# A rope product's halves are swapped by ScalarE on the way out of PSUM, instead of by VectorE in its two multiplies

## The chip, the cores and the metric

The kernel runs on one core of a Trainium2 chip. The metric is the device time of the execution in microseconds, the median of several runs. One more execution is taken by the hardware profiler, and all rows below are from that one.

## What is computed

One attention block and one feed-forward block over 1024 tokens of width 512, each behind a layer norm and with a residual. The attention has 32 query heads of width 128 in 8 groups; keys K and values V are shared by the four heads of a group. Each head has besides them a latent key and value of its own (LK, LV), and attends twice with the same query: to K, V and to LK, LV. The queries, the keys and the latent keys pass through the rotary embedding (rope), which is where the change lies:

```
def _rotate_half(x):
    h = x.shape[-1] // 2
    return jnp.concatenate([-x[..., h:], x[..., :h]], axis=-1)

def _apply_rope(x, cos, sin):
    return x * cos[None, None] + _rotate_half(x) * sin[None, None]
...
q = _apply_rope(q, cos, sin)
k = _apply_rope(k, cos, sin)
lk = _apply_rope(lk, cos, sin)
...
attn = _causal_attn(q, k, v, SCALE)
lat = _causal_attn(q, lk, lv, SCALE)
...
return attn @ w_o + lat @ w_lo
```

## The kernel before

Every engine runs its own list of instructions, written out by hand in the order in which it is to work, and waits on semaphores. The matmuls are in fp32r with each operand split into a high and a low half (`_hi`, `_lo`), so a product takes three matmuls (L433 to L435). ScalarE makes the high half by a copy (L721 is the one line of all its copies), and VectorE or GpSimd subtracts it from the source for the low half (L997 and L1070 on VectorE, L1213 on GpSimd).

**A head** has four windows: w = 0 and 1 are K, V for the first and the second half of the queries (512 tokens each), w = 2 and 3 the same for LK, LV. A window has 4 or 8 blocks of keys (slots s). In each slot TensorE computes score tiles of the next window, one *piece* of other work, the transposes of the exponentials (L496) and the product of a block with the values in bankO. VectorE takes the row maxima (L991), ScalarE the exponentials (L780). Transposed blocks pass as PT_hi (ScalarE) and PT_lo (VectorE), or PTD_hi and PTD_lo for the last block of a window. The transposes of block j + 2 wait until PT_lo of block j is written, because they write the same bankT.

**Pieces** are the projections of what the next window or head needs. Each writes 512 columns of PSUM, in bankX or in the second half of scores[1]. LK0 and LK1 (the two halves of the tokens) come in w = 0, slots 0 and 1; Q0 of the next head in w = 2, slot 3; Q1 in w = 3, slot 0, in the same bankX right after it. In the last head of a group K0, K1 and V0 of the next group take slots 0 to 2 of w = 2 as well. Before TensorE writes a bank again, it waits (`bank_x_taken`) until the last piece in it was read; for a rope piece this is the semaphore `rope_raw`.

**A rope product** passes through four engines. ScalarE copies the bank to one of three slots of `rot` and raises `rope_raw` (`rope_take`). VectorE (`rotate`) multiplies each half of the partitions by sine and writes it to the other half of `rot_half`, which has two places (L1007, L1008), and raises `rope_half`. GpSimd multiplies `rot` by cosine in place (L1219), adds `rot_half` (L1221) and raises `rope_sum`. ScalarE copies the high half to QT, KT or LKT (`rope_high`), GpSimd subtracts for the low half (L1213) and raises `rope_lo`, for which the score tiles wait. In ScalarE's list the take of LK stands in front of the slot's PT_hi and exponentials; that of Q and K stands behind the exponentials and in front of PT_hi. In VectorE's list the rotation of Q stands in front of PT_lo of the same slot; that of LK and K stands one slot later, behind PT_lo. There are 144 such products: 64 LK, 64 Q and 16 K, four of them before the first head.

Of the kernel before, what the change touches and what calls it, by code (L numbers as in the profile page):

```python
# [9 lines left out]
ALU = mybir.AluOpType  # L10
# [6 lines left out]
H, KVH, HD = 32, 8, 128  # L17
# [5 lines left out]
HALF = HD // 2  # L23
# [6 lines left out]
RING = 3  # L30
# [70 lines left out]
def attn_ffn_kernel(nc, x_in, w_q, w_k, w_v, w_o, w_lq, w_lk, w_lv, w_out_latent, W, b, A, B, router_W, router_b,  # L101
                    cos_in, sin_in, mask_in, ident_in, pick_in,
                    averaged_in, out, inverses):
    with ExitStack() as ctx:
        def sb(name, shape, dt=F32):
            return ctx.enter_context(nc.sbuf_tensor(name, shape, dt))
# [5 lines left out]
        def sem(name):  # L112
            return ctx.enter_context(nc.semaphore(name))
# [3 lines left out]
        sin = sb("sin", [P, S])  # L117
# [17 lines left out]
        rot_half = sb("rot_half", [P, 2, CH])  # L135
        rot = sb("rot", [P, RING, CH])
# [22 lines left out]
        banksX = [bankX[:, :], scores[1][:, 1, :]]  # L159
# [13 lines left out]
        rope_raw, rope_half, rope_cos = sem("rope_raw"), sem("rope_half"), sem("rope_cos")  # L173
        rope_sum, rope_lo, o_lo, w_lo, cleared = (sem("rope_sum"), sem("rope_lo"), [sem("o_lo0"), sem("o_lo1")], sem("w_lo"),
                                                  sem("cleared"))
# [542 lines left out]
        def _(act):  # L718

            def copy(place, src):  # L720
                return act.activation(place, src, ACT.Copy)  # L721
# [36 lines left out]

                weights_hi(None, no % 2, g * (LOADS_PER_GROUP // 2) + (no // 2 + 1), places)

            def rope_take(n_x, no, slot, bank=0):

                if not (isinstance(no, int) and no < RING):
                    act.wait_ge(rope_lo, no - (RING - 1))
                act.wait_ge(x_ready, n_x)
                copy(rot[:, slot, :], banksX[bank] if isinstance(bank, int) else bank).then_inc(rope_raw, 1)

            def rope_high(no, slot, place):
                act.wait_ge(rope_sum, no + 1)
# [29 lines left out]
            def group_of_heads(g, last):  # L799
                for hh, w, more in windows(g, last):  # L800
# [3 lines left out]
                    for s in range(BLOCKS[w]):  # L804
                        name, n = pieces_of(w, hh, more).get(s, ("", 0))
                        if name == "LK":
                            rope_take(n_piece(g, hh, w, s), rope_no(g, hh, name, n), rope_no(0, hh, name, n) % RING,
                                      piece_bank(hh, w, s, more))
# [7 lines left out]
                        if name in ("Q", "K"):  # L816
                            rope_take(n_piece(g, hh, w, s), rope_no(g, hh, name, n), rope_no(0, hh, name, n) % RING,
                                      piece_bank(hh, w, s, more))
# [63 lines left out]
            def first_take(p):  # L882
                rope_take((1, 2, 5, 6)[p], p, p % RING, four[p % 2])
# [45 lines left out]
        def _(dve):  # L929
# [70 lines left out]
            def rotate(no, slot, n, place=None):  # L1000

                half = n if place is None else place
                if not (isinstance(no, int) and no < 2):
                    dve.wait_ge(rope_sum, no - 1)
                dve.wait_ge(rope_raw, no + 1)
                t = slice(n * CH, (n + 1) * CH)
                dve.tensor_tensor(rot_half[0:HALF, half, :], rot[HALF:HD, slot, :], sin[HALF:HD, t], ALU.mult)  # L1007
                dve.tensor_tensor(rot_half[HALF:HD, half, :], rot[0:HALF, slot, :], sin[0:HALF, t], ALU.mult)\  # L1008
                    .then_inc(rope_half, 1)

            def value_copy(n_x, n, bank=0):
                dve.wait_ge(x_ready, n_x)
# [13 lines left out]
            def piece(g, hh, w, s, name, n, bank):  # L1026
                n_x = n_piece(g, hh, w, s)
                if name in ROPE:
                    rotate(rope_no(g, hh, name, n), rope_no(0, hh, name, n) % RING, n)
                elif name in ("V", "LV"):  # L1030
                    value_copy(n_x, n, bank)
                elif name in ("VT", "LVT"):

                    value_lo(vt_no(g, hh, name, n) + 3, V if name == "VT" else LV, n, bank)
                else:
                    add_out(n_x, n_free(g, hh, w, s), n + (TPC if name == "OUT1" else 0), bank)
# [93 lines left out]
            for i in range(TPC, NT):  # L1130
                normalised_lo(0, i)
            rotate(0, 0, 0, 0)
            rotate(1, 1, 0, 1)
            latent_lo(0)
            dve.wait_ge(mask_made, 1)
# [66 lines left out]
            for n in range(2):  # L1202
                dve.wait_ge(f_hi, ND + 3 + n)
                t = slice(n * CH, (n + 1) * CH)
# [114 lines left out]
def shape_constants():  # L1319

    inv_freq = (1.0 / THETA ** (np.arange(0, HD, 2, dtype=np.float32) / HD)).astype(np.float32)
    freqs = np.outer(np.arange(S, dtype=np.float32), inv_freq).astype(np.float32)
    cos = np.tile(np.cos(freqs).T, (2, 1)).astype(np.float32)
    sin = np.concatenate([np.sin(freqs).T, -np.sin(freqs).T], 0).astype(np.float32)
    mask = np.zeros((P, S), np.float32)
    mask[:, S - P:] = np.where(np.tril(np.ones((P, P), bool)), 0.0, MASKED)
    pick = (np.arange(P)[:, None] // R == np.arange(E)[None, :]).astype(np.float32)
    token = np.arange(NT)[None, :] * P + np.arange(P)[:, None]
    averaged = ((token >= Q_START) & (token < Q_STOP)).astype(np.float32)
    return {"cos": cos, "sin": sin, "mask": mask, "ident": np.eye(P, dtype=np.float32), "pick": pick,  # L1330
            "averaged": averaged}
# [19 lines left out]
```

## Time and profile before

| | us |
|---|---|
| median of 3 runs (2121.29 to 2122.29) | 2121.59 |
| the profiled execution | 2121.26 |
| its span, first to last instruction | 2119.5 |
| TensorE busy | 2066.4 (97%) |
| VectorE busy | 1531.2 (72%) |
| ScalarE busy | 1203.0 (57%) |
| GpSimd busy | 894.4 (42%) |

TensorE's granted clock is 0.998 of full speed over the span. PE in the rows is TensorE's matmul, PEld its weight load, DVE VectorE, ACT ScalarE, POOL GpSimd. Ends of matmuls are modelled and overlap the next one. One ordinary head lasts about 60 us, and the last of a group about 73.

### The profile page before, as it was taken

The numbers are of one execution on the slowest core, as the hardware profiler recorded it, in microseconds if no ns is written. First come the engines' busy times: TensorE is split into PE (matmuls) and PEld (weight loads), VectorE is DVE, ScalarE is ACT, GpSimd is POOL, SyncE is SP. The second block draws the span as 40 slices with busy tenths as digits, with TensorE's granted clock in tenths as the row PEclk, the third lists the DMA queues.
The fourth block names the chain that finished last, engine by engine and source line by source line (L and its number), as shares of the span: only waits on it lengthen the run. The fifth ranks groups of instructions, "written<-read, shape, count | busy, mean of one in ns | idle before, by whom it ended". The sixth has DMA issues, their size and how long they took to land.

```text
span 2119.5 us, 32469 instructions
## 1 busy us (share of the span) xinstructions
PE 2066.4 (97%) x11236; PEld 1754.4 (83%) x11236; DVE 1531.2 (72%) x2946; ACT 1203.0 (57%) x2507; POOL 894.4 (42%) x691
## 2 busy tenths in 40 slices
PE   6999999999999999999999999999999999999989
PEld 5888888888888888888888888888888888888877
DVE  7777777776777677777677767777677777777775
ACT  4566555565566555566556555556646555555641
POOL 4433453444544353444443345444354345444411
PEclk9999999999999999999999999999999999999999
DMA  2111111111111111111111111111111111111121
GB/s 97 42 37 38 45 32 40 29 42 47 31 34 40 33 41 37 36 42 32 37 42 37 35 47 32 27 42 37 47 31 37 42 27 47 31 42 36 38 51 40
DMA packets 101937, 83.72 MB, mean 39 GB/s; under 512 B 28296, under 2 KB 73992, under 8 KB 101776
## 3 DMA queue, kind: packets, MB, share of 16 engines
q1 hardware_dynamic: 101776, 81.65, 15.1%
q8 instruction: 91, 1.49, 0.3%
q14 instruction: 70, 0.57, 0.1%
HBM read 79.26 MB, written 2.36 MB: 39 GB/s over the span
## 4 chain that ended last, share of the span: by engine, by line
PE 69%; DVE 15%; POOL 6%; issue 6%; ACT 4%; DMA 0%; SPq 0%; ACTq 0%; DVEq 0%
PE scores L433 9%; PE scores L435 9%; PE scores L434 9%; PE bankT L496 7%; PE bankX L433 6%; PE bankX L435 6%; PE bankX L434 6%; PE bankO L433 5%; PE bankO L435 5%; PE bankO L434 5%; DVE rot_half L1008 4%; DVE rot_half L1007 4%; DVE PT_lo L997 2%; POOL rot L1219 2%; POOL rot L1221 2%
## 5 line engine op out<-in xcount | busy, mean ns | idle before, releaser
L721 ACT ACTIVATE PT_hi<-bankT 128x512 fp32r<-128x512 f32 (+2 forms) x640 | 336.3, 532 | 389.1 <-PE bankO L435 326.9
L997 DVE TENSOR_TENSOR PT_lo<-bankT,PT_hi 128x512 fp32r<-128x512 f32 (+2 forms) x640 | 386.7, 607 | 194.7 <-ACT PT_hi L721 189.7
L780 ACT ACTIVATE probs<-probs,nmax 128x128 f32<-128x128 f32 (+7 forms) x512 | 395.5, 774 | 134.3 <-DVE nmax L991 133.7
L991 DVE CUSTOM_DVE_ANT_0 probs<-scores,mask 128x128 f32<-128x128 f32 (+7 forms) x512 | 381.3, 750 | 55.5 <-PE scores L435 54.4
L496 PE MATMUL bankT<-ident,probs 128*128 128x128 f32 x2304 | 379.1, 273 | 22.2 <-DVE PT_lo L997 20.0
L496 PEld LDWEIGHTS bankT<-ident,probs 128*128 128x128 f32 x2304 | 285.2, 140 | 90.6 <-DVE PT_lo L997 35.6
L1213 POOL TENSOR_TENSOR OT_lo<-o_raw,OT_hi 128x512 fp32r<-128x512 f32 x64 | 99.9, 1561 | 417.6 <-ACT OT_hi L721 417.6
L1219 POOL TENSOR_TENSOR rot<-rot,cos 128x512 f32<-128x512 f32 x144 | 186.2, 1293 | 199.4 <-DVE rot_half L1008 199.4
L721 ACT ACTIVATE OT_hi<-o_raw 128x512 fp32r<-128x512 f32 x128 | 147.0, 1148 | 145.5 <-DVE o_raw L1062 145.5
L1221 POOL TENSOR_TENSOR rot<-rot,rot_half 128x512 f32<-128x512 f32 x144 | 204.1, 1417 | 11.3
L1007 DVE TENSOR_TENSOR rot_half<-rot,sin 64x512 f32<-64x512 f32 x144 | 110.0, 764 | 85.4 <-ACT rot L721 81.7
L1008 DVE TENSOR_TENSOR rot_half<-rot,sin 64x512 f32<-64x512 f32 x144 | 153.7, 1067 | 2.0
L721 ACT ACTIVATE rot<-bankX 128x512 f32<-128x512 f32 x140 | 83.3, 595 | 109.7 <-PE bankX L435 108.7
L433 PE MATMUL scores<-LKT_hi,QT_lo 128*128 128x384 f32 (+4 forms) x384 | 138.4, 361 | 2.4
L433 PE MATMUL bankO<-PT_hi,LV_lo 128*128 128x512 f32 (+2 forms) x320 | 136.0, 425 | 0.3
L433 PE MATMUL bankO<-PT_hi,V_lo 128*128 128x512 f32 (+2 forms) x320 | 136.1, 425 | 0.0
L433 PE MATMUL scores<-KT_hi,QT_lo 128*128 128x384 f32 (+4 forms) x384 | 133.8, 348 | 1.5 <-POOL KT_lo L1213 1.2
L1024 DVE TENSOR_TENSOR acc<-scores,acc 128x512 f32<-128x512 f32 x130 | 89.6, 690 | 62.7 <-PE scores L435 59.9
L435 PE MATMUL scores<-KT_hi,QT_hi 128*128 128x384 f32 (+4 forms) x384 | 132.0, 344 | 0.0
L435 PE MATMUL scores<-LKT_hi,QT_hi 128*128 128x384 f32 (+4 forms) x384 | 131.9, 343 | 0.0
L434 PE MATMUL scores<-KT_lo,QT_hi 128*128 128x384 f32 (+4 forms) x384 | 131.7, 343 | 0.0
L434 PE MATMUL scores<-LKT_lo,QT_hi 128*128 128x384 f32 (+4 forms) x384 | 131.7, 343 | 0.0
(254 smaller groups left out, 5170.5 us busy)
## 6 DMA issues: line engine op xcount, KB each, us to landing
inv_b<-inverses SPq DMA_DIRECT2D x128, 256.0 KB, 3.9
stage<-in_L_attn_w_q SPq DMA_DIRECT2D x32, 256.0 KB, 4.8
stage<-in_L_attn_w_lv SPq DMA_DIRECT2D x32, 256.0 KB, 2.8
stage<-in_L_attn_w_o SPq DMA_DIRECT2D x32, 256.0 KB, 4.9
stage<-in_L_attn_w_lo SPq DMA_DIRECT2D x32, 256.0 KB, 2.6
acc<-in_L_attn_hidden_states SPq DMA_DIRECT2D x8, 256.0 KB, 4.8
stage<-in_L_attn_w_k SPq DMA_DIRECT2D x8, 256.0 KB, 5.1
stage<-in_L_attn_w_v SPq DMA_DIRECT2D x8, 256.0 KB, 5.4
```

Of the source, the lines that this page charges most:

```text
L433: pe.matmul(place, left[1], right[0], start=start, stop=False)
L434: pe.matmul(place, left[0], right[1], start=False, stop=False)
L435: return pe.matmul(place, left[0], right[0], start=False, stop=stop)
L496: mm = pe.transpose(bankT[j % 2][:, t * P:(t + 1) * P], probs[c][:, at:at + P], ident[:, :])
L721: return act.activation(place, src, ACT.Copy)
L780: act.activation(prob_tile(c, t), prob_tile(c, t), ACT.Exp, bias=nmax[:, c, t:t + 1], scale=-1.0, accum_out=rsum[:, c, t:t + 1]).then_inc( ...
L991: dve.tensor_tensor_reduce(place, src, tile_view(mask[:, S - width:S], c), -SCALE, -MASKED, ALU.add, ALU.min, nmax[:, c, t:t + 1]).then_in ...
L997: dve.tensor_tensor(pt_place(1, hh, w, j), bankT[j % 2][:, block_columns(c, j):CH], f32(pt_place(0, hh, w, j)), ALU.subtract).then_inc(pt_ ...
L1007: dve.tensor_tensor(rot_half[0:HALF, half, :], rot[HALF:HD, slot, :], sin[HALF:HD, t], ALU.mult)
L1008: dve.tensor_tensor(rot_half[HALF:HD, half, :], rot[0:HALF, slot, :], sin[0:HALF, t], ALU.mult)\
L1219: pool.tensor_tensor(rot[:, slot, :], rot[:, slot, :], cos[:, chunk(n)], ALU.mult).then_inc(rope_cos, 1)
L1221: pool.tensor_tensor(rot[:, slot, :], rot[:, slot, :], rot_half[:, half, :], ALU.add).then_inc(rope_sum, 1)
```

## The change

ScalarE reads the bank three times: the upper half of the partitions to the lower half of `rot_half`, the lower half to the upper, and then the whole to `rot` as before, where `rope_raw` is raised. VectorE multiplies all of `rot_half` by sine in one instruction, in place. The sine table has its sign in the other half. The wait for `rope_sum` of two products before, which protects the place in `rot_half`, moves from VectorE to ScalarE.

```diff
-            def rope_take(n_x, no, slot, bank=0):
-
-                if not (isinstance(no, int) and no < RING):
+            def rope_take(n_x, no, slot, bank=0, place=None):
+
+                half = no % 2 if place is None else place
+                src = banksX[bank] if isinstance(bank, int) else bank
+                if no >= 2:
+                    act.wait_ge(rope_sum, no - 1)
+                if no >= RING:
                     act.wait_ge(rope_lo, no - (RING - 1))
                 act.wait_ge(x_ready, n_x)
-                copy(rot[:, slot, :], banksX[bank] if isinstance(bank, int) else bank).then_inc(rope_raw, 1)
+                copy(rot_half[0:HALF, half, :], src[HALF:HD, :])
+                copy(rot_half[HALF:HD, half, :], src[0:HALF, :])
+                copy(rot[:, slot, :], src).then_inc(rope_raw, 1)
...
                 half = n if place is None else place
-                if not (isinstance(no, int) and no < 2):
-                    dve.wait_ge(rope_sum, no - 1)
                 dve.wait_ge(rope_raw, no + 1)
                 t = slice(n * CH, (n + 1) * CH)
-                dve.tensor_tensor(rot_half[0:HALF, half, :], rot[HALF:HD, slot, :], sin[HALF:HD, t], ALU.mult)
-                dve.tensor_tensor(rot_half[HALF:HD, half, :], rot[0:HALF, slot, :], sin[0:HALF, t], ALU.mult)\
-                    .then_inc(rope_half, 1)
+                dve.tensor_tensor(rot_half[:, half, :], rot_half[:, half, :], sin[:, t], ALU.mult).then_inc(rope_half, 1)
...
-    sin = np.concatenate([np.sin(freqs).T, -np.sin(freqs).T], 0).astype(np.float32)
+    sin = np.concatenate([-np.sin(freqs).T, np.sin(freqs).T], 0).astype(np.float32)
```

## Rows read from the trace of the kernel before

**Rows 1.** The page: busy time of each engine, share of the span, instructions.

```profile
PE 2066.4 (97%) x11236; PEld 1754.4 (83%) x11236; DVE 1531.2 (72%) x2946; ACT 1203.0 (57%) x2507; POOL 894.4 (42%) x691
```

**Rows 2.** Waits: who waited <- for whom: us in total, times, longest.

```profile
PE bankT L496 <- DVE PT_lo L997: 20.0, 32, 1.1
...
PEld scores L433 <- POOL LKT_lo L1213: 16.4, 32, 0.5
...
PEld bankX L433 <- ACT rot L721: 3.0, 7, 0.4
```

**Rows 3.** Instructions on tile rot_half: duration in ns min/median/max, first and last start.

```profile
L1007 DVE TENSOR_TENSOR rot_half<-rot,sin x144: 686/687/1810, 26.1 to 2008.1; 64x512 f32<-64x512 f32 x144
L1008 DVE TENSOR_TENSOR rot_half<-rot,sin x144: 684/685/1690, 26.8 to 2008.8; 64x512 f32<-64x512 f32 x144
```

**Rows 4.** Timeline of TensorE, 907 to 918: start us, duration us, instruction [idle before <-releaser].

```profile
909.09 0.48 PE L433 MATMUL bankX<-xnT_hi,Wq_lo 128*128 128x512 f32 x1
...
911.70 0.39 PE L435 MATMUL bankX<-xnT_hi,Wq_hi 128*128 128x512 f32 x1
...
915.14 0.40 PE L434 MATMUL scores<-Wlo_lo,OT_hi 128*128 128x512 f32 x1
915.37 0.40 PE L435 MATMUL scores<-Wlo_hi,OT_hi 128*128 128x512 f32 x1
916.27 0.66 PE L496 MATMUL bankT<-ident,probs 128*128 128x128 f32 x4 [0.50 <-DVE PT_lo L997]
...
917.46 0.28 PE L433 MATMUL scores<-KT_hi,QT_lo 128*128 128x256 f32 x1
```

**Rows 5.** Timeline of ScalarE, the same stretch.

```profile
908.20 0.60 ACT L721 ACTIVATE rot<-bankX 128x512 f32<-128x512 f32 x1 [0.60 <-PE bankX L435]
908.69 1.33 ACT L721 ACTIVATE PT_hi<-bankT 128x512 fp32r<-128x512 f32 x2
...
912.74 0.60 ACT L721 ACTIVATE rot<-bankX 128x512 f32<-128x512 f32 x1
...
914.39 0.60 ACT L721 ACTIVATE PT_hi<-bankT 128x512 fp32r<-128x512 f32 x1 [0.54 <-PE bankO L435]
914.89 0.62 ACT L721 ACTIVATE QT_hi<-rot 128x512 fp32r<-128x512 f32 x1
```

**Rows 6.** Timeline of VectorE, the same stretch.

```profile
909.61 0.69 DVE L1008 TENSOR_TENSOR rot_half<-rot,sin 64x512 f32<-64x512 f32 x1
910.32 0.69 DVE L997 TENSOR_TENSOR PT_lo<-bankT,PT_hi 128x512 fp32r<-128x512 f32 x1
910.93 0.68 DVE L1062 TENSOR_TENSOR o_raw<-bankO,inv_b 128x512 f32<-128x512 f32 x1
...
915.52 1.29 DVE L997 TENSOR_TENSOR PT_lo<-bankT,PT_hi 128x512 fp32r<-128x512 f32 x2
```

**Rows 7.** Timeline of GpSimd, the same stretch.

```profile
915.59 1.27 POOL L1213 TENSOR_TENSOR QT_lo<-rot,QT_hi 128x512 fp32r<-128x512 f32 x1 [2.54 <-ACT QT_hi L721]
```

**Rows 8.** Timeline around LK1, 933 to 944, of ScalarE, VectorE and TensorE.

```profile
933.35 0.60 ACT L721 ACTIVATE rot<-bankX 128x512 f32<-128x512 f32 x1 [1.46 <-PE bankX L435]
...
934.15 0.29 DVE L997 TENSOR_TENSOR PTD_lo<-bankT,PTD_hi 128x128 fp32r<-128x128 f32 x1 [0.30 <-ACT PTD_hi L721]
...
935.89 1.23 DVE L991 CUSTOM_DVE_ANT_0 probs<-scores,mask 128x1024 f32<-128x1024 f32 x1
...
938.23 0.60 PE L496 MATMUL bankT<-ident,probs 128*128 128x128 f32 x4
...
943.13 0.40 PE L435 MATMUL bankO<-PT_hi,V_hi 128*128 128x512 f32 x1
943.60 0.39 PE L433 MATMUL scores<-LKT_hi,QT_lo 128*128 128x256 f32 x1
```

**Rows 9.** Timeline at the end of a group: K1's copy, V's first matmul.

```profile
1029.57 0.60 ACT L721 ACTIVATE rot<-bankX 128x512 f32<-128x512 f32 x1
...
1030.22 0.50 PE L433 MATMUL bankX<-xnT_hi,Wv_lo 128*128 128x512 f32 x1
```

## The prediction

> **What bounds the kernel now.** I read the page's busy line first, then the waits, then the instructions of one head in order of time. TensorE is busy 97% of the span and VectorE 72% [rows 1], so the question for every edit is whether it moves a matmul. A record of TensorE overlaps the next one: a 512-column matmul is booked with 0.40 us, but the next starts 0.23 us after it (915.14 to 915.37) [rows 4]. So a hole in TensorE is read from start to start, not from its busy time. In the heads the holes that matter are few. Once a head transposes wait for VectorE's PT_lo, 32 times for 20.0 us [rows 2]; in the head at 908 that is a start at 916.27 where 915.60 (915.37 + 0.23) was possible, 0.67 us [rows 4]. Once a head the first latent score waits for GpSimd's LKT_lo, 32 times [rows 2]: 943.13 to 943.60 is 0.47 where 0.23 is the step, 0.24 us lost [rows 8]. In front of bankX, waits for ScalarE's copy are only 7, and short [rows 2]. The heads repeat this closely; the head at 908 stands for the 24 heads that fetch a next query without new keys, and 7 more also make K and V.
>
> The second thing to see is how near to TensorE the copy already is. Of a head's four rope products, Q0 and Q1 follow each other through the same bankX. Q0's copy runs 908.20 to 908.80, and TensorE starts Q1 there at 909.09 [rows 5, 4]. Where it does wait (1029.57 + 0.60, matmul at 1030.22 [rows 9], once per group) the signal takes 0.05. The slack is then 0.24 us. The same gap of 0.28 or 0.29 is there at 30 of the 31 Q0 (the first at 89.89, the last at 1979.12), 0.05 at one. LK0, LK1 and K0 leave more room than two copies take.
>
> **VectorE's part.** Two 64x512 multiplies of 0.69 us go, 144 times each; that is their median, and single ones last up to 1.8 [rows 3], stretched when GpSimd works at the same time. One 128x512 multiply comes. The trace has the same operation at half the partitions for 0.69, as long as 128x512 PT_lo, so partitions are free and I price it at 0.69. The old pair does not overlap its neighbours: 909.61 to 910.32 is a step of 0.71, while PT_lo to o_raw is 0.61 for 0.69 [rows 6]. I take 0.61 for the new one, so VectorE gets back 1.42 - 0.61 = 0.80 us a product. Bounds: 0.71 gained if it keeps the long step, 1.7 where it escapes a stretch. It is in place and also uses two SBUF inputs, so a stretch to 1.7 stays possible. The Trainium skill (VectorE: DVE Perf Modes, Two Vector instructions with no wait between them) says that an instruction whose start quadrant differs from the last one's waits for everything before it; the steps of 0.71 and 0.61 agree, and it says nothing of ScalarE.
>
> **ScalarE's part.** Two 64x512 copies from PSUM come in front of the one that was there, and `rope_raw`, which frees bankX and starts VectorE, comes only with the third. A copy takes 0.60 [rows 5]; by VectorE's half-height rows a half is no cheaper than a whole. ScalarE's copies overlap when they start at partition 0: 908.20 to 908.69, a step of 0.49 [rows 5]. No row shows ScalarE moving between partitions 0 and 64. The price of the pair lies between 2 x 0.49 = 0.98 (overlap kept) and 2 x 0.62 = 1.24 (none, as VectorE's rows with just these halves). I take 1.24, because the row with the same change of partitions is the nearer one; both ends stay in. The Trainium skill (ScalarE: Activation LUTs, What ACT_TABLE_LOAD costs) gives an immediate-operand ACTIVATE 186 ns + 0.833 ns an element and an overlap of about 93 ns back to back, whatever the partitions; as an estimate that is 0.52 a copy, 1.04 for the pair, and the sum would be near the first rival's. The added wait for `rope_sum` of two products before costs nothing in the heads: that product was added up several us earlier; VectorE loses the same wait.
>
> **Q0 and Q1, with 1.24.** Q0's third copy ends 908.20 + 1.24 + 0.60 = 910.04, TensorE gets bankX at 910.09 instead of 909.09: a new hole of 1.00 us, ahead of the whole Q1 projection, its score and output work. Now what is late next. Q1's last matmul ended 911.70 + 0.39; with 1.00 and 0.10 for the signal ScalarE can take it at 913.19. ScalarE itself is late too: VectorE's multiply starts 1.24 later but gives 0.80 back, so o_raw and OT_hi come 0.44 later, and the take, 912.74 before [rows 5], starts near 913.3. Its three copies end at 913.3 + 1.84 = 915.15. VectorE multiplies at 915.25 and reaches PT_lo at 915.86 instead of 915.52 [rows 6]. Before, TensorE's transposes followed PT_lo's start by 0.75, so they can start at 916.61; TensorE by itself is there at 915.60 + 1.00 = 916.60. So the old hole of 0.67 disappears in the new one, and 0.34 us remain.
> Behind it stands Q0's high and low half. ScalarE's PT_hi at 914.39 waited for TensorE; it is now pushed to 915.53 by the copies, QT_hi from 914.89 to 916.03 [rows 5], GpSimd's QT_lo (0.70 behind QT_hi's start, 1.27 long [rows 7]) to 916.73, ending 918.00. The score that reads it began at 917.46 [rows 4] and now begins at 918.05: 0.59 us late in all. 24 x 0.59 = 14.2 us.
>
> **LK1.** Before it ScalarE idles 1.46 us, which hides LK0's extra copies. LK1's own move PTD_hi behind them: VectorE's PTD_lo from 934.15 to about 935.38 (933.35 + 1.24 + 0.49 + 0.27 + 0.03), and the 1024-wide maximum follows 1.74 - 0.80 = 0.94 later, at 936.32 instead of 935.89 [rows 8]. Its exponential is late by 0.43; the transposes that read it (938.23, four of them [rows 8]) have perhaps 0.1 to spare. TensorE loses about 0.33 and then no longer waits for LKT_lo, 0.24: net 0.09, 32 x 0.09 = 3 us.
>
> **K1, V and the group ends (7).** V's first matmul already waits for K1's copy [rows 9] and moves by the whole 1.24. Q0 to Q1 adds up to 1.00. Holes of the same stretch (the largest kind of wait for PT_lo is 1.1 [rows 2]) swallow part; between 1.2 and 2.2 I take 1.4: 10 us. Start: TensorE works without a hole while the first products are taken, nothing. End: no ropes.
>
> **Sum.** 14.2 + 3 + 10 = 27 us. The profiled execution took 2121.26 with a span of 2119.5, 0.3 below the median of 2121.59. Forecast 2148, 1.3% slower.
>
> **Rivals.**
> *ScalarE overlaps the three copies* (0.98). For it: every pair of ScalarE copies in the trace overlaps. Against: VectorE's pair with these halves does not. Q1 then starts 0.74 late, the transposes 0.07, and the score behind QT_lo 0.19: 24 x 0.19 = 4.6. At LK1 the maximum is 0.17 late, less than slack and LKT_lo's 0.24 together: 32 x -0.17 = -5. Group ends 7 x 1.25 = 9. Time 2130.
> *VectorE's relief decides, faster.* The mechanism is the 0.80 us returned in front of PT_lo. It wins only if the two half copies together cost under the 0.24 of slack; then the holes close, 24 x 0.67 + 7 x 1.2 + 32 x 0.24 = 32 us, 2089. The balance tips near 0.8 for the pair, 0.4 a copy. For it: only half of the partitions are written. Against: half-height VectorE instructions cost as much as full ones.
> *No change.* The pair at about 0.8, or the halves overlapped and the group ends swallowing all of it: 2118 to 2126.
> *ScalarE becomes a second bound.* If in-place multiplies stretch to 1.7 beside GpSimd where the old pair ran at 0.69, VectorE gains nothing, maxima and PT_lo are 0.3 to 0.8 later in each head: 10 to 25 us on top, 2158 to 2172.
>
> **How the numbers follow.** Forecast case 50%, with a range of its own 2140 to 2157; overlapped copies 29%; no change 7%; faster 8%; second bound 6%. A difference under 0.2% cannot be told from none here. Range: down to 2125, below the overlapped case's own error of 5 us, and up to 2158. Faster 0.08, same 0.07, slower 0.85.
>
> **What would show it.** In the new trace: three ScalarE rows of bankX for each product, and their step (0.62 or 0.49); VectorE's multiply once, 0.69 long; first matmul of Q1 waiting for ScalarE's rot about 1.0 us, 31 times; the wait of transposes for PT_lo nearly gone; a new wait of the scores for QT_lo; the wait for LKT_lo gone. The forecast is wrong if a half copy is much cheaper than 0.49, if QT_lo is not late, or if VectorE's stretches grow.

## The result and the profile after

The changed kernel takes 2147.24 us (median of 4, 2146.86 to 2147.62) against 2121.44 for the kernel before in the same comparison: ratio 1.0123, 95% interval 1.0105 to 1.014. The forecast was 2148, range 2125 to 2158. The profiled execution has a span of 2145.6 instead of 2119.5.

The page, part 1, busy time of each engine [rows 1 before]:

```profile
PE 2074.2 (97%) x11236; PEld 1758.5 (82%) x11236; DVE 1350.2 (63%) x2802; ACT 1378.4 (64%) x2795; POOL 879.6 (41%) x691
```

The change did what it says: 181 us of work left VectorE and 175 came to ScalarE. The two engines are nearly as busy as each other now, and the kernel is slower. The waits tell why (who <- for whom: us in total, times, longest) [rows 2 before]:

```profile
PEld bankX L433 <- ACT rot L721: 42.2, 38, 1.7
...
PE bankX L433 <- ACT rot L721: 32.6, 38, 1.3
PEld scores L433 <- POOL QT_lo L1215: 21.9, 31, 1.4
...
PEld scores L433 <- DVE nmax L997: 15.0, 58, 0.5
...
PE scores L433 <- POOL QT_lo L1215: 6.9, 7, 1.0
...
PEld bankT L496 <- DVE PT_lo L1003: 0.7, 2, 0.5
```

TensorE waited for ScalarE's copy 7 times before, now 38 times (31 Q1 and 7 V). The wait for PT_lo, once a head before, is gone, and so is the one for LKT_lo. A wait for QT_lo has come, 31 times. Score tiles wait for a row maximum (nmax) in 58 records instead of 26; the row of the kernel before is:

```profile
PEld scores L433 <- DVE nmax L991: 6.2, 26, 0.5
```

The same place as [rows 4 to 7], one ordinary head, timeline of TensorE (start, duration, instruction, idle before and its releaser):

```profile
919.55 0.60 PE L496 MATMUL bankT<-ident,probs 128*128 128x128 f32 x4
920.90 0.50 PE L433 MATMUL bankX<-xnT_hi,Wq_lo 128*128 128x512 f32 x1 [0.75 <-ACT rot L721]
...
927.18 0.39 PE L435 MATMUL scores<-Wlo_hi,OT_hi 128*128 128x512 f32 x1
927.41 0.60 PE L496 MATMUL bankT<-ident,probs 128*128 128x128 f32 x4
...
928.31 0.40 PE L435 MATMUL bankO<-PT_hi,LV_hi 128*128 128x512 f32 x1
928.77 0.39 PE L433 MATMUL scores<-KT_hi,QT_lo 128*128 128x256 f32 x1
929.00 0.28 PE L434 MATMUL scores<-KT_lo,QT_hi 128*128 128x256 f32 x1
```

and of ScalarE, VectorE and GpSimd there:

```profile
919.04 1.20 ACT L721 ACTIVATE rot_half<-bankX 64x512 f32<-64x512 f32 x2 [0.62 <-PE bankX L435]
920.25 0.60 ACT L721 ACTIVATE rot<-bankX 128x512 f32<-128x512 f32 x1
920.75 1.08 ACT L721 ACTIVATE PT_hi<-bankT 128x512 fp32r<-128x512 f32 x2
...
926.73 0.62 ACT L721 ACTIVATE QT_hi<-rot 128x512 fp32r<-128x512 f32 x1
...
920.88 0.69 DVE L1011 TENSOR_TENSOR rot_half<-rot_half,sin 128x512 f32<-128x512 f32 x1 [4.05 <-ACT rot L721]
921.49 0.68 DVE L1003 TENSOR_TENSOR PT_lo<-bankT,PT_hi 128x512 fp32r<-128x512 f32 x1
...
926.49 1.28 DVE L1003 TENSOR_TENSOR PT_lo<-bankT,PT_hi 128x512 fp32r<-128x512 f32 x2
...
927.42 1.29 POOL L1215 TENSOR_TENSOR QT_lo<-rot,QT_hi 128x512 fp32r<-128x512 f32 x1 [3.10 <-ACT QT_hi L721]
```

The two half copies take 1.20 (919.04 to 920.25), with no overlap; the copy behind them gives way after 0.50, as before. TensorE gets bankX 1.86 us after the first copy starts, before 0.89. From there on the transposes at 927.41 start with no hole behind 927.18, and the score at 928.77 has one of 0.23.

At the end of a group, TensorE's timeline [rows 9 before]:

```profile
1042.97 0.50 PE L433 MATMUL bankX<-xnT_hi,Wv_lo 128*128 128x512 f32 x1 [1.34 <-ACT rot L721]
...
1062.40 0.39 PE L433 MATMUL scores<-KT_hi,QT_lo 128*128 128x256 f32 x1 [0.98 <-POOL QT_lo L1215]
```

Around LK0 and LK1, ScalarE's, VectorE's and TensorE's [rows 8 before]:

```profile
941.76 1.21 ACT L721 ACTIVATE rot_half<-bankX 64x512 f32<-64x512 f32 x2
...
943.47 0.38 ACT L721 ACTIVATE PT_hi<-bankT 128x256 fp32r<-128x256 f32 x1
...
944.77 1.20 ACT L721 ACTIVATE rot_half<-bankX 64x512 f32<-64x512 f32 x2
...
943.88 0.42 DVE L1003 TENSOR_TENSOR PT_lo<-bankT,PT_hi 128x256 fp32r<-128x256 f32 x1 [2.11 <-ACT PT_hi L721]
944.22 0.95 DVE L997 CUSTOM_DVE_ANT_0 probs<-scores,mask 128x768 f32<-128x768 f32 x1
...
946.78 0.29 DVE L1003 TENSOR_TENSOR PTD_lo<-bankT,PTD_hi 128x128 fp32r<-128x128 f32 x1 [0.59 <-ACT PTD_hi L721]
946.99 0.68 DVE L1011 TENSOR_TENSOR rot_half<-rot_half,sin 128x512 f32<-128x512 f32 x1
947.59 1.22 DVE L997 CUSTOM_DVE_ANT_0 probs<-scores,mask 128x1024 f32<-128x1024 f32 x1
...
945.23 0.19 PEld L433 LDWEIGHTS scores<-KT_hi,QT_lo 128*128 128x128 f32 x1 [0.26 <-DVE nmax L997]
```

and LK0 before the change:

```profile
930.24 0.58 ACT L721 ACTIVATE rot<-bankX 128x512 f32<-128x512 f32 x1
...
931.51 0.96 DVE L991 CUSTOM_DVE_ANT_0 probs<-scores,mask 128x768 f32<-128x768 f32 x1
...
933.73 0.39 PE L433 MATMUL scores<-KT_hi,QT_lo 128*128 128x512 f32 x1
```

Before, the maximum over 768 columns started 1.27 us behind LK0's copy and had ended, 932.47 at the latest, more than 1 us ahead of the next score tile, which did not wait. Now LK0's copies stand in front of PT_hi, PT_lo and this maximum. It starts 2.46 us behind the first of them, and the score tile waits for it.

From one Q0 copy to the next in ScalarE's timeline, the four heads of a group took 59.7, 59.7, 69.0 and 64.4 us; now 60.2, 60.2, 70.7 and 64.7. An ordinary head lost 0.5 us, a whole group 3.1. From the first Q0 to the last the loss is 23 us; of the other 3, 1.2 lie ahead of the first (its copy starts at 91.06 instead of 89.89) and the rest behind the last. These 3 cannot simply be put down to the change. TensorE's granted clock ahead of the first Q0 is 1.00 of full speed (2.4 GHz) in the trace before and 0.98 in the one after, and behind the last 0.96 and 0.95; between them it is 1.00 in both. Run 6, whose edit leaves the start alone, has 0.98 there too and is as late: the last matmul of the first Q0 projection starts at 90.7 us, at 90.5 in the changed kernel and at 89.4 before.

### The profile page after: what moved, and what is told of

Its sections match the earlier page's. It is cut to its first block, busy times and chain, and to the rows that moved or that the text cites. A ratio compares the mean times of both kernels' runs of the same rounds, so it can differ in the third digit from the quotient of the medians.

```text
span 2145.6 us, 32472 instructions
## 1 busy us (share of the span) xinstructions
PE 2074.2 (97%) x11236; PEld 1758.5 (82%) x11236; DVE 1350.2 (63%) x2802; ACT 1378.4 (64%) x2795; POOL 879.6 (41%) x691
## 4 chain that ended last, share of the span: by engine, by line
PE 85%; ACT 7%; DVE 3%; issue 2%; POOL 2%; DMA 0%; SPq 0%; ACTq 0%; DVEq 0%
PE scores L433 12%; PE scores L435 11%; PE scores L434 11%; PE bankT L496 9%; PE bankX L433 8%; PE bankX L435 7%; PE bankX L434 7%; PE bankO L435 6%; PE bankO L433 6%; PE bankO L434 5%; ACT rot_half L721 3%; POOL QT_lo L1215 2%; ACT rot L721 1%; ACT OT_hi L721 1%; ACT QT_hi L721 1%
## 5 line engine op out<-in xcount | busy, mean ns | idle before, releaser
L721 ACT ACTIVATE PT_hi<-bankT 128x512 fp32r<-128x512 f32 (+2 forms) x640 | 331.4, 533 | 334.2 <-PE bankO L435 274.4
L721 ACT ACTIVATE rot_half<-bankX 64x512 f32<-64x512 f32 x280 | 166.2, 594 | 73.4 <-PE bankX L435 66.4
L1011 DVE TENSOR_TENSOR rot_half<-rot_half,sin 128x512 f32<-128x512 f32 x144 | 113.2, 786 | 144.2 <-ACT rot L721 144.2
L1223 POOL TENSOR_TENSOR rot<-rot,rot_half 128x512 f32<-128x512 f32 x144 | 196.7, 1366 | 11.3
L433 PE MATMUL scores<-KT_hi,QT_lo 128*128 128x384 f32 (+4 forms) x384 | 140.7, 366 | 10.1 <-POOL QT_lo L1215 6.9
L1026 DVE TENSOR_TENSOR acc<-scores,acc 128x512 f32<-128x512 f32 x130 | 89.6, 689 | 62.4 <-PE scores L435 59.7
L1215 POOL TENSOR_TENSOR QT_lo<-rot,QT_hi 128x512 fp32r<-128x512 f32 x64 | 82.6, 1290 | 110.5 <-ACT QT_hi L721 110.5
```

Source lines behind the costliest of these rows:

```text
L433: pe.matmul(place, left[1], right[0], start=start, stop=False)
L1011: dve.tensor_tensor(rot_half[:, half, :], rot_half[:, half, :], sin[:, t], ALU.mult).then_inc(rope_half, 1)
L1215: return pool.tensor_tensor(place, src, f32(hi), ALU.subtract)
L1223: pool.tensor_tensor(rot[:, slot, :], rot[:, slot, :], rot_half[:, half, :], ALU.add).then_inc(rope_sum, 1)
```

## The experiments

Each was measured beside the kernel before, on the same chip as it; ratios are to it, with their 95% intervals. Where an ordinary head is given and nothing else is said, it is counted in TensorE's timeline from the last matmul of one Q0 projection to that of the next, 59.7 us in the kernel before.

**1. VectorE's part alone.** One multiply, one copy; the halves are not swapped.

```diff
-                dve.tensor_tensor(rot_half[0:HALF, half, :], rot[HALF:HD, slot, :], sin[HALF:HD, t], ALU.mult)
-                dve.tensor_tensor(rot_half[HALF:HD, half, :], rot[0:HALF, slot, :], sin[0:HALF, t], ALU.mult)\
-                    .then_inc(rope_half, 1)
+                dve.tensor_tensor(rot_half[:, half, :], rot[:, slot, :], sin[:, t], ALU.mult).then_inc(rope_half, 1)
```

> VectorE's part alone: one 128x512 multiply of rot by sine, without the swap of halves; ScalarE takes the bank with one copy, as before. Theory (a late bank and late copies cost the time, VectorE's relief is real but covered): with the relief and no added copies the waits of the transposes for PT_lo and of the scores for LKT_lo close, 24 x 0.67 + 7 x 1.2 + 32 x 0.24 = 32 us, so 2089 (2085 to 2096). Rival (VectorE is off TensorE's path, its relief is worth nothing): 2121, as before.

Measured: 2096.83 us, ratio 0.9879 (0.9864 to 0.9894). VectorE's relief is worth 24 us, so the rival falls. It is 8 short of 2089 and 1 outside the theory's range, and the waits name what came in its place:

```profile
PEld scores L433 <- POOL QT_lo L1211: 22.0, 31, 1.4
```

**2. ScalarE's part alone.** The half copies go to a spare tile, VectorE works as before.

```diff
+                if no >= 2:
+                    act.wait_ge(rope_sum, no - 1)
+                copy(spare[0:HALF, no % 2, :], src[HALF:HD, :])
+                copy(spare[HALF:HD, no % 2, :], src[0:HALF, :])
                 copy(rot[:, slot, :], src).then_inc(rope_raw, 1)
```

> ScalarE's part alone: the two half copies go to a spare tile, VectorE rotates with its two multiplies as before. Theory: the copies cost more than the whole change, because nothing is given back: at Q1 the transposes come 1.9 us late (24 x 1.9 = 46), at LK1 the exponential is 1.2 late (32 x 1.1 = 36), at a group's end about 3 (7 x 3 = 22): 2220 (2195 to 2240). Rival (the whole loss is TensorE's wait for the bank, 31 x 1.0): 2150, like the changed kernel.

Measured: 2225.13 us, ratio 1.0481 (1.0463 to 1.0498). The waits:

```profile
PEld bankT L497 <- DVE PT_lo L1003: 47.2, 40, 1.7
PEld bankX L434 <- ACT rot L722: 41.0, 38, 1.6
PEld bankT L497 <- ACT probs L786: 33.6, 36, 1.2
```

The copies alone cost 104 us, four times the change; the time is inside the theory's range. The bank is the smaller part of it. An ordinary head takes 62.7 us, 3.0 more than before. From start to start in TensorE's timeline, 0.96 of these are the bank, 0.71 a longer wait for PT_lo, 0.94 the exponential behind LK1, and most of the rest OT_lo and the score tile behind LK0, 0.2 each. The same 38 waits for the bank are in the changed kernel; the waits for PT_lo and for the exponential are not (2 and 5 records), and the difference between the two kernels is the 0.8 us a product that VectorE saves.

**3. Whole copies instead of halves.** As many copies and twice the elements, but all from and to partition 0; the halves are not swapped.

```diff
-                copy(rot_half[0:HALF, half, :], src[HALF:HD, :])
-                copy(rot_half[HALF:HD, half, :], src[0:HALF, :])
+                copy(rot_half[:, half, :], src)
+                copy(spare[:, no % 2, :], src)
```

> The changed kernel, but the two half copies are whole copies of 128 partitions from and to partition 0 (the halves are not swapped, the second goes to a spare tile): as many instructions, twice the elements, no change of partitions. Theory (a ScalarE copy that starts at other partitions than the last cannot overlap it, 0.61 a step instead of 0.49): steps of 0.49, 0.25 us less for each product, near 2131 (2127 to 2136). Rival (three reads of one bank, or the count of copies, make the step 0.61): 2147, as changed.

Measured: 2129.34 us, ratio 1.0039 (1.0026 to 1.0052), as the theory says. ScalarE's timeline:

```profile
911.68 0.60 ACT L722 ACTIVATE rot_half<-bankX 128x512 f32<-128x512 f32 x1 [0.62 <-PE bankX L436]
912.17 0.59 ACT L722 ACTIVATE spare<-bankX 128x512 f32<-128x512 f32 x1
912.65 0.60 ACT L722 ACTIVATE rot<-bankX 128x512 f32<-128x512 f32 x1
```

The steps are 0.49 and 0.48. Three reads of one bank in a row overlap, so the rival falls. Each copy lasts 0.60 with 64 partitions or 128; the lost overlap costs 0.24 us a product and 18 us over the kernel, two thirds of the whole loss. The run takes away two things at once, the move between partitions 0 and 64 and the half height. That the move is the one that costs the overlap is argued and not shown: no run has half copies that start where the last one did.

**4. Q1 in the other bank.**

```diff
-            return (sorted(pieces_of(w, hh, more)).index(s) + (w == 1)) % 2 if w in (1, 3) else 0
+            return (sorted(pieces_of(w, hh, more)).index(s) + (w == 1 or more)) % 2 if w in (1, 3) else 0
```

> The changed kernel, but Q1 (and with it every piece of the fourth window, in turn) goes to the other bank, so that TensorE doesn't wait for Q0's copies. Theory (behind the bank stands a chain of the same length, ScalarE's three copies of Q1, then PT_lo and QT_hi): the wait of 0.75 for the bank goes, and nearly the same time comes back as waits for PT_lo and QT_lo: 2143 to 2147. Rival (the bank wait is the cost): 31 x 0.9 = 28 us less, 2119.

Measured: 2137.92 us, ratio 1.0078 (1.0063 to 1.0093), between the two, 5 below the theory's range. TensorE's timeline of an ordinary head has three short waits where there was one for the bank:

```profile
920.31 0.47 PE L433 MATMUL bankX<-Wo_hi,OT_lo 128*128 128x512 f32 x1 [0.16 <-DVE OT_lo L1072]
...
922.20 0.66 PE L496 MATMUL bankT<-ident,probs 128*128 128x128 f32 x4 [0.27 <-DVE PT_lo L1003]
...
923.74 0.39 PE L433 MATMUL scores<-KT_hi,QT_lo 128*128 128x256 f32 x1 [0.18 <-POOL QT_lo L1215]
```

From one QT_hi to the next an ordinary head takes 60.15 us, against 60.2 in the changed kernel: there the time came back entirely, as the theory says, and the rival, 28 us less, falls. A group end is shorter by about 0.9, where I had counted nothing, and that makes 6 of the 9 us.

**5. The kernel before, with VectorE's rotation of Q1 behind PT_lo.**

```diff
-                        if s in here and here[s][0] not in ("LK", "K"):
+                        if s in here and here[s][0] not in ("LK", "K") and here[s] != ("Q", 1):
                             piece(g, hh, w, s, *here[s], piece_bank(hh, w, s, more))
                         if s + 2 < BLOCKS[w]:
                             block_lo(g, hh, w, s + 2)
+                        if s in here and here[s] == ("Q", 1):
+                            piece(g, hh, w, s, *here[s], piece_bank(hh, w, s, more))
```

> The kernel before, with VectorE's rotation of Q1 behind PT_lo of the same slot instead of in front of it; nothing of the change. Theory (in an ordinary head TensorE lost 0.67 us to PT_lo behind this rotation, and QT_lo is next, 0.2 to 0.4 later than it would then be wanted, as in the run of VectorE's part alone): 24 x 0.4 = 10 and about 5 at the group ends, 2106 (2100 to 2112). Rival (the hole only moves to a later block, whose PT_lo is now behind the rotation): 2121.

Measured: 2119.59 us against 2122.21, ratio 0.9988 (0.9978 to 0.9997): the order alone is worth nearly nothing, and the time is 8 us above the theory's range. The theory was right in what comes next and wrong in its size; the score now waits for QT_lo and gives back 0.64 of the 0.73 us that the transposes no longer lose:

```profile
916.04 0.39 PE L433 MATMUL scores<-KT_hi,QT_lo 128*128 128x256 f32 x1 [0.37 <-POOL QT_lo L1215]
```

**6. The same, and QT_hi one slot earlier.**

```diff
-            highs = [{(0, 3): ("LK", 0), (1, 0): ("LK", 1), (3, 1): ("Q", 0), (3, 3): ("Q", 1)} for _ in range(GROUP)]
-            highs[GROUP - 1].update({(2, 3): ("K", 0), (3, 0): ("K", 1)})
+            highs = [{(0, 3): ("LK", 0), (1, 0): ("LK", 1), (3, 0): ("Q", 0), (3, 3): ("Q", 1)} for _ in range(GROUP)]
+            highs[GROUP - 1].update({(2, 3): ("K", 0), (3, 0): ("K", 1), (3, 1): ("Q", 0)})
```

> The last kernel, and ScalarE makes QT_hi of Q0 one slot earlier in ordinary heads, in front of PT_hi of the next block instead of behind it. Theory (QT_lo is what is late next): the waits for QT_lo go there, 24 x 0.25 = 6 us less than the last one, near 2099 (2094 to 2105). Rival (QT_lo is not binding without the relief): as the last one.

Measured: 2122.58 us, ratio 1.0003 (0.9993 to 1.0012), 3 us above run 5, where 6 less were expected: a miss. The hole moved once more, to the transposes one slot later, which wait for the next PT_lo, now behind the rotation:

```profile
918.97 0.55 PE L496 MATMUL bankT<-ident,probs 128*128 128x128 f32 x3 [0.51 <-DVE PT_lo L997]
```

That was the rival of run 5. While VectorE needs 1.4 us for Q1 at this place, each of the three orders that were tried puts something of the stretch behind it.

**7. The changed kernel with its late steps moved.** Q1 in the other bank (run 4) and VectorE's order of run 5; in Q1's slot ScalarE makes PT_hi and Q0's QT_hi in front of the copies.

```diff
+                        if (name, n) == ("Q", 1):
+                            block_hi(g, hh, w, s + 2)
+                            if hh < GROUP - 1:
+                                act.wait_ge(scored, tiles_made(g, hh, w))
+                                rope_high(rope_no(g, hh, "Q", 0), rope_no(0, hh, "Q", 0) % RING,
+                                          QT[0][:, (hh + 1) % 2, 0:CH])
                         if name in ("Q", "K"):
```

> The changed kernel with its three late things moved: Q1 in the other bank, and in Q1's slot PT_hi and Q0's QT_hi in front of ScalarE's copies, PT_lo in front of VectorE's multiply. Theory (the change costs by where the copies stand, ScalarE has the time for them): the waits for bank, PT_lo and QT_lo of ordinary heads go, V's wait for K1's copies stays, 7 x 1.3: about 2108 (2100 to 2118). Rival (the added 175 us of ScalarE's work cost wherever they stand): over 2130.

Measured: 2121.58 us against 2122.21, ratio 0.9998 (0.9988 to 1.0007). The whole loss of the change is gone with ScalarE's work still there, so the rival falls; but the kernel is almost 4 us above the theory's range, 13 above its 2108, and not faster than before. Part of what stays is at the group's end, TensorE's timeline:

```profile
1030.95 0.50 PE L433 MATMUL bankX<-xnT_hi,Wv_lo 128*128 128x512 f32 x1 [1.34 <-ACT rot L721]
...
1049.52 0.38 PE L433 MATMUL scores<-KT_hi,QT_lo 128*128 128x256 f32 x1 [0.98 <-POOL QT_lo L1223]
```

The larger part is in the ordinary heads, which I had not foreseen. They take 59.5 us; in run 10, which has VectorE's relief without the copies, they take 58.5. The difference stands at three places of TensorE's timeline: 0.4 at the output product that reads OT_lo, 0.2 at the transposes behind Q1, 0.2 at the score tile behind LK0. The first is shown here:

```profile
855.35 0.47 PE L433 MATMUL bankX<-Wo_hi,OT_lo 128*128 128x512 f32 x1 [0.16 <-DVE OT_lo L1078]
```

Q0's copies make o_raw, a head's output before it is split, start 3.04 us behind the first of them instead of 2.73, and OT_hi and OT_lo follow it.

**8. The change for LK alone.** Q and K as before; the sign of their sine product is the other one.

```diff
-                copy(rot_half[0:HALF, half, :], src[HALF:HD, :])
-                copy(rot_half[HALF:HD, half, :], src[0:HALF, :])
+                if swap:
+                    copy(rot_half[0:HALF, half, :], src[HALF:HD, :])
+                    copy(rot_half[HALF:HD, half, :], src[0:HALF, :])
```

> The change for LK0 and LK1 alone (64 of 144 products); Q and K are taken and rotated as before (the sign of their sine product is the other one). Theory: 32 x 0.09 = 3 us over the kernel before, 2124 (2119 to 2129), the wait for LKT_lo gone and a small one for the exponential in its place. Rival (each product's copies cost alike): 64/144 of 26 us = 12, 2133.

Measured: 2120.50 us against 2122.21, ratio 0.9991 (0.9982 to 1.0001), inside the theory's range and clear of the rival. 64 of the 144 products cost nothing, if not a little less than nothing. The waits show two effects that nearly cancel: the 32 records of a wait for LKT_lo are gone, and those for a row maximum rise from 26 to 57:

```profile
PEld scores L433 <- DVE nmax L998: 14.4, 57, 0.5
```

Behind the first scores of a head, the rest of it takes 49.6 us instead of 49.7, and so it does in the changed kernel. The loss belongs to Q and K.

**9. The changed kernel of run 7, but K as before.** VectorE rotates K0 and K1 in two multiplies, GpSimd subtracts for them.

```diff
-                                      piece_bank(hh, w, s, more))
+                                      piece_bank(hh, w, s, more), swap=name == "Q")
...
-                            rope_add(*k_no[0], 0)
-                            rope_add(*k_no[1], 1)
+                            rope_add(*k_no[0], 0, op=ALU.subtract)
+                            rope_add(*k_no[1], 1, op=ALU.subtract)
```

> The last kernel with the change in its new places (Q1 in the other bank, PT_hi, QT_hi and PT_lo in front of it), but K0 and K1 are taken with one copy and rotated by VectorE in two multiplies as before the change, and GpSimd subtracts instead of adds for them, because the sine table has the other sign. Theory (what was left of the change's cost there is V's wait for K1's copies, 1.34 a group): 7 x 1.2 = 8 us less than that kernel's 2121.6, 2113 (2110 to 2117), faster than the kernel before by 0.4%. Rival (that wait is swallowed by the wait for QT_lo at the group's end, 0.98 there): 2120 to 2122.

Measured: 2113.36 us against 2120.15, ratio 0.9961 (0.9947 to 0.9974), as the theory says. It computes what the kernel before does and is faster than it and than the changed kernel. The waits for bankX are down to a few short ones:

```profile
PEld bankX L433 <- ACT rot L721: 3.4, 8, 0.4
```

**10. VectorE's part alone, and QT_hi one slot earlier** (the edits of runs 1 and 6; halves not swapped).

> VectorE's part alone (one multiply without the swap of halves, one copy by ScalarE), and ScalarE makes QT_hi of Q0 one slot earlier in ordinary heads. Theory (the part alone stayed at 2097 instead of 2089 because the scores then wait for QT_lo, 24 x 0.3): those waits go, 7 us less, 2090 (2086 to 2093). Rival (PT_hi, now behind QT_hi, makes PT_lo of the next block late, as it did without VectorE's relief): 2097.

Measured: 2085.91 us against 2120.15, ratio 0.9838 (0.9825 to 0.9851). That is 4 below the theory and just below its range. The 8 us missing in run 1 were the wait for QT_lo of ordinary heads, which take 58.5 us instead of run 1's 58.9; its records fall from 31 to the 7 of the group ends:

```profile
PEld scores L433 <- POOL QT_lo L1211: 9.9, 7, 1.4
```

The edit of run 6, worth nothing on its own, is worth 8 to 10 us once the rotation is short.

## Why the prediction was right, step by step

The time is 0.8 us from the forecast, and the likeliest case is the one that happened. That it came so close is luck: the heads lost 23 us where 27 were forecast, and the 3 us outside them, where nothing was forecast, go with a lower granted clock at the two ends of the kernel. Two terms were off by 6 and 2 us in opposite directions.

*ScalarE's price.* The choice of 1.24 for the two half copies over 0.98 decided between the forecast and 2130. Measured 1.20; run 3, which has the 0.98, gave 2129. The 1.24 was taken from VectorE's rows for the same halves; the trace after shows ScalarE losing its overlap on them too. The Trainium skill (ScalarE: Activation LUTs, What ACT_TABLE_LOAD costs) says that ACTIVATEs back to back overlap by about 93 ns. It names no condition on partitions. Run 3's copies agree with it, 0.60 long and 0.49 or 0.48 apart; the half copies of the changed kernel do not overlap at all.

*VectorE's price.* 0.61 a step: 920.88 to 921.49. Its median is 0.69; 9 of the 144 last over 0.9, up to 1.69, each while GpSimd is at work, and the mean is 0.79. The case of the second bound did not come.

*Q0 and Q1*, counted at 0.59 a head. The bank came 0.97 late (counted 1.00). PT_lo was only 0.13 late (0.34), from the first copy 7.45 us instead of 7.32; TensorE by itself was later than that, so it made no difference. QT_lo was late as described. From Q0's first copy to the first score with the new query it was 9.26 us before and is 9.73, 0.47 late where 0.59 were counted. Behind this wait the next matmul starts 0.23 later (928.77 to 929.00) and not 0.12 as before, which nobody had counted. So TensorE is 0.59 late in all when it goes on: 10.58 us from the last matmul of Q0's projection to the last of that score instead of 9.99. The 24 x 0.59 = 14.2 us came out, by two errors that cancel.

*LK0 and LK1*, counted at 0.09. This term has the wrong sign. The 1024-wide maximum was 0.28 late instead of 0.43, counted from LK1's first copy, and the transposes behind its exponential lost 0.03 us and not 0.33. LK0's copies, put at nothing because ScalarE idles behind them, cost 0.2 by way of the earlier maximum at 944.22. Against both stand 0.34 that TensorE no longer loses for LKT_lo (0.24 at the score and 0.10 at the matmul behind it). A head gains 0.1: -3 us where +3 were forecast. Run 8, with nothing but these products changed, has the same 0.1. The first rival's 2130, which run 3 met with 2129, hid errors of the same kind: 0.38 instead of 0.19 for Q0 and Q1, -0.31 instead of -0.17 for LK.

*Group ends*, counted at 1.4 and 0.09. A group lost 3.1 us, three ordinary heads 1.5 of it, so 1.6, or 1.7 without LK's gain. V's first matmul is 1.23 late (its wait is 1.34 as a record); the wait for QT_lo, 0.98, which I used for ordinary heads only, is here too and replaces the old one for PT_lo. 7 of them make 12, where 10 were forecast. 14 - 3 + 12 = 23 us, and the remaining 3 lie before the first Q0 and behind the last, where I had counted nothing.

*The faster rival* was right about its mechanism, and its condition, a pair of half copies under 0.24 us, was not met: runs 1 and 10 show 24 us behind VectorE's relief alone and 34 with QT_hi moved as well, where 32 were worked out. What the copies cost with nothing given back is the 104 us of run 2. Neither number can be read from the sum of 26: the parts overlap on the same waits, and 104 - 24 is not 26.

What stays open: whether the half height or the move between partitions takes ScalarE's overlap; what the places of run 7 would do for the kernel before, all together, since only runs 5 and 6 tried two of them there; and whether a swap without ScalarE could reach the 2086 of run 10.

## What to carry to other kernels

Where an engine's copy frees a PSUM bank for TensorE, price an added read of the bank by the slack between the copy's end and the next matmul into it, not by the engine's load: ScalarE was at 57% and had the time, 0.24 us of slack did not. Then follow every engine's list behind the added work to the next wait, because a hole removed in one place is filled by what was covered by it: runs 4, 5 and 6 each removed a wait in the ordinary heads and gained 9, 3 and 0 us. Work handed to an engine with time to spare wants new places in that engine's order; with them, and with K left as it was, the change went from 1.2% slower to 0.4% faster.

## What the runs showed of the hardware

ScalarE's copies of 512 columns from PSUM overlap by 0.11 us (0.60 long, a step of 0.49, run 3) when each covers all partitions from 0 on. The 64-partition copies that change between partitions 0 and 64 do not (1.20 for two, the changed kernel): behind each of its 288 half copies the next copy starts 0.01 us after the end. Half the partitions cost as much as all, 594 ns median against 598. VectorE showed the same, a step of 0.71 behind the half-height multiplies before and 0.61 behind the whole one after.

Behind a 256-column matmul that was late for its data the next one starts 0.1 us later than behind one that was not: 0.23 from start to start at 928.77 in the changed kernel, 0.12 for the same matmuls at 917.46 in the kernel before.
